# Field rows of a tile numbered 3i+r in place of 39r+i, with a separate load for the transposes

## What is computed

```
e  = stack([tbl_f[ids[:, f]] for f in range(39)], axis=1)          # 512 x 39 x 16
x1 = einsum('bid,bjd,ijh->bhd', e, e,  W0.reshape(39, 39, 128))    # 512 x 128 x 16
x2 = einsum('bid,bjd,ijh->bhd', e, x1, W1.reshape(39, 128, 128))
z  = sum(concatenate([x1, x2], axis=1), axis=-1)                   # 512 x 256
h  = maximum(concatenate([z, dense_ctx], 1) @ W_top1 + b_top1, 0)
h  = maximum(h @ W_top2 + b_top2, 0)
y  = h @ W_top3                                                    # 512 x 1
```

## Time and profile before

| | us |
|---|---|
| median of 3 runs | 597.44 (595.48 to 598.78) |
| profiled execution, its own time | 593.85 |
| its span in the trace | 592.0 |
| TensorE busy | 285.3 (48%) |
| VectorE busy | 168.1 (28%) |
| ScalarE busy | 137.9 (23%) |
| GpSimd busy | 154.1 (26%) |

### The profile page before, as it was taken

One profiled execution on the slowest core, in us unless ns is written; L12 is line 12 of the kernel. 1 busy time (PEld: TensorE's weight loads), 2 busy tenths in 40 slices (PEclk: granted clock), 3 DMA queues, 4 the chain that ended last, 5 costly groups with the idle time before them and its releaser, 6 DMA issues.

```text
span 592.0 us, 3817 instructions
## 1 busy us (share of the span) xinstructions
PE 285.3 (48%) x1132; PEld 219.6 (37%) x1132; DVE 168.1 (28%) x267; ACT 137.9 (23%) x252; POOL 154.1 (26%) x164
## 2 busy tenths in 40 slices
PE   3132450542617182643717183754736272746588
PEld 1011240331405172532615072642634161635367
DVE  4032230231414142231413142232414042232400
ACT  2011130230413122231413122231403122231421
POOL 6777733205060513214060513314000000000000
PEclk9999995575655557696955767685657577685879
DMA  3242255232232222222222222223212121122100
GB/s 75 45 109 64 76 141 120 79 98 67 80 60 80 57 81 56 78 66 68 77 60 79 54 81 57 80 67 74 72 57 81 50 79 51 76 64 74 67 0 2
DMA packets 59450, 41.50 MB, mean 70 GB/s; under 512 B 37323, under 2 KB 42699, under 8 KB 59430
## 3 DMA queue, kind: packets, MB, share of 16 engines
q1 hardware_dynamic: 54310, 39.94, 22.1%
q0 software_dynamic: 5120, 1.32, 3.8%
HBM read 36.65 MB, written 1.97 MB: 65 GB/s over the span
## 4 chain that ended last, share of the span: by engine, by line
SPq 86%; PE 4%; DMA 4%; issue 3%; POOL 2%; ACT 1%; DVE 0%; DVEq 0%
SPq L261 41%; SPq L286 17%; SPq L248 14%; SPq L247 8%; DMA second<-fields 3%; SPq L258 2%; SPq L272 2%; PE tower L542 2%; POOL gathered L310 2%; SPq L267 1%; SPq L271 1%; SPq L274 1%; PE tower L560 0%; DMA fields<-gathered 0%; SPq L275 0%
## 5 line engine op out<-in xcount | busy, mean ns | idle before, releaser
L310 POOL DMA_INDIRECT gathered<-table,rows x160 | 153.9, 962 | 254.1 <-DMA fields<-gathered 205.7
L340 DVE TENSOR_TENSOR prod<-first,second 117x512 f32<-117x512 f32 x112 | 77.6, 693 | 380.4 <-issue 194.8
L403 ACT CAST prod_hi<-prod 117x512 fp32r<-117x512 f32 x112 | 69.2, 618 | 244.2 <-DVE prod L340 244.2
L512 PE MATMUL sums<-prod_hi,w_hi 117*128 117x512 f32 x112 | 73.5, 656 | 101.6 <-DVE prod_lo L348 101.4
L497 PE MATMUL ring<-ident_f,first 39*128 39x39 f32 x64 | 10.3, 309 | 187.7 <-DMA first<-fields 187.7
L497 PEld LDWEIGHTS ring<-ident_f,first 39*128 39x128 f32 x64 | 8.0, 211 | 194.7 <-DMA first<-fields 194.7
L512 PEld LDWEIGHTS sums<-prod_hi,w_hi 117*128 117x128 f32 x112 | 28.7, 256 | 132.9 <-DVE prod_lo L348 100.4
L348 DVE TENSOR_TENSOR prod_lo<-prod,prod_hi 117x512 fp32r<-117x512 f32 x112 | 76.7, 685 | 0.1
L542 PE MATMUL tower<-dots,w_sb 128*128 128x128 f32 x312 | 62.1, 338 | 0.0
L542 PEld LDWEIGHTS tower<-dots,w_sb 128*128 128x128 f32 x312 | 59.0, 250 | 6.2 <-issue 0.2
L513 PE MATMUL sums<-prod_lo,w_hi 117*128 117x512 f32 x112 | 59.3, 529 | 0.0
(11 more groups left out here) (77 smaller groups left out, 157.5 us busy)
## 6 DMA issues: line engine op xcount, KB each, us to landing
second<-fields SPq DMA_DIRECT2D x112, 234.0 KB
first<-fields SPq DMA_DIRECT2D x16, 234.0 KB
gathered<-table,rows POOLq DMA_INDIRECT x160, 3.4
diag<-columns SPq DMA_DIRECT2D x128, 20.0 KB, 1.9
fields<-gathered SPq DMA_DIRECT2D x16, 80.0 KB, 10.1
wt_sb<-wt SPq DMA_DIRECT2D x2, 512.0 KB, 10.8
fields<-gathered SPq DMA_DIRECT2D x16, 40.0 KB, 10.2
w0a<-w_ij SPq DMA_DIRECT2D x1, 409.5 KB
```

The source lines that it names most:

```text
L310: pool.indirect_dma_start(gathered[:, k % NGATHER, q, :], None, table, bass.IndirectOffsetOnAxis(ap=rows[:, k, q:q + 1], axis=0)).then_inc ...
L340: nc.vector.tensor_tensor(prod[:, m % NPROD, :], first[:, k % 2, :], second[:, k % 2, t, :], ALU.mult)\
L403: nc.scalar.copy(prod_hi[:, m % NPART, :], prod[:, m % NPROD, :]).then_inc(hi_ready, 1)
L512: pe.matmul(to, w0_hi[:, t, :], hi, start=(t == 0), stop=False)
```

## The change

The rows of a tile are numbered p = 3i + r. In DRAM, the source of a tile load is described by three nested counts. Before, the outermost count is 3 (r) and the next 39 (i); in the change the outermost is 39 and the next 3. The destination has 117 partitions in both, and the bytes and the number of runs of 2 KB are the same. Row i of `first` was field i for the first 39 rows, and the transposes read these. Now three rows in a row hold the same field, so a ninth load of 39 rows, `turned`, brings the fields once more for the transposes; it is issued behind the load of tile 0. To make room for it, NGATHER is 3 in place of 4. The weight rows are sorted on the host by the new table.

```diff
@@ pair_tiles
-            i, shift = p % FIELDS, RUN * t + p // FIELDS
+            i, shift = p // RUN, RUN * t + p % RUN
@@ build
-        NPROD, NPART, NGATHER, NRING = 5, 7, 4, 4
+        NPROD, NPART, NGATHER, NRING = 5, 7, 3, 4
+        turned = sb("turned", [FIELDS, 2, COLS])
+        turned_in = [sem(f"turned_in{i}") for i in range(2)]
@@ load_pairs
                 sp.dma_start(first[:, at, :],
-                             bass.AP(fields.tensor, row, [[0, RUN], [COLS, FIELDS], [1, COLS]])).then_inc(first_in[at], 16)
+                             bass.AP(fields.tensor, row, [[COLS, FIELDS], [0, RUN], [1, COLS]])).then_inc(first_in[at], 16)
                 for t in range(TILES):
                     sp.dma_start(second[:, at, t, :],
-                                 bass.AP(fields.tensor, row + RUN * t * COLS, [[COLS, RUN], [COLS, FIELDS], [1, COLS]]))\
+                                 bass.AP(fields.tensor, row + RUN * t * COLS, [[COLS, FIELDS], [COLS, RUN], [1, COLS]]))\
                         .then_inc(second_in[t][at], 16)
+                    if t == 0:
+                        sp.dma_start(turned[:, at, :], bass.AP(fields.tensor, row, [[COLS, FIELDS], [1, COLS]]))\
+                            .then_inc(turned_in[at], 16)
@@ fields_by_column
-                pe.wait_ge(first_in[k % 2], 16 * (k // 2 + 1))
+                pe.wait_ge(turned_in[k % 2], 16 * (k // 2 + 1))
-                                      first[0:FIELDS, k % 2, P * s:P * s + P], ident_f[0:FIELDS, 0:FIELDS])
+                                      turned[:, k % 2, P * s:P * s + P], ident_f[0:FIELDS, 0:FIELDS])
```

## The result

| us | before | changed |
|---|---|---|
| median | 596.46 | 329.8 (328.04 to 332.64, 4 runs) |
| profiled execution, its own time | 593.85 | 328.04 |
| its span | 592.0 | 326.2 |

The ratio is 0.5533, with an interval of 0.5486 to 0.5579. The direction and the cause were forecast, the size was not: 284 was predicted, and 329.8 lies above the range of 262 to 316. On three later occasions the same kernel took about 400 us, as did most of its variants. So the ratio is that of one calm occasion out of four. All readings of the change itself come from undisturbed executions, or from blocks between spells.

What follows compares the result with a forecast made beforehand. The prediction took the kernel before as bound by eight tile loads draining at 3.2 us each. GpSimd's line to the last loads, 233.4, plus 14.3 + 30.6 + 3 gave 281.3, outside the span 283.2, forecast 284 us; range 262 to 316.

Steps and rivals of the forecast that it cites:

- part 1: Tile loads with 39 outermost: spread over 13 DMA engines in place of about three, 0.74 us a load for 3.2.
- 0.74 us a load: Drain of one tile load on 13 engines, 3.2 x 3/13; as long as its undisturbed issue of 0.69 to 0.76 us.
- at 288 a load takes 0.83: Rival: DMA engines at 288 GB/s or TensorE's waits set 15 to 15.5 us a block, 305 us in all; chance 0.12.
- the share of 0.97: DMA engines' busy share while the weights arrive, at 288 GB/s; read as 16 engines, the upper bound for tile loads.
- SyncE's sum of 13.5: SyncE's issues for one block: 12.7 us for fields, copies, tile loads and waits, plus 0.75 for the ninth load.
- L3: Start of block 3's tile loads on SyncE: forecast at 69.5 us, L2 + 13.5 + 2.
- L1: Start of block 1's tile loads on SyncE: forecast at 37.3 us, after its gathers landed at 30.9.
- L2: Start of block 2's tile loads on SyncE: forecast at 54 us, including two weight loads and fields behind them.
- is the bound by a hair: GpSimd's gathers, slowed beside VectorE, were to take 14.0 us a block, just over SyncE's 13.5.
- GpSimd held up fully: Rival: each gather waits out the VectorE operation it meets, 16.7 us a block, 321 us; 0.15 for 298 to 321.
- Part 2: Ninth load, for the transposes: 0.75 us of SyncE's queue, its landing hidden with 2.8 us to spare before the copies.
- Part 3: Three gather buffers: gathers wait for the fields of block k - 2 or k - 4, met by about a period; no cost.

Runs made afterwards that it cites:

- three_outer: Changed kernel with rows numbered 39r+i and 3 outermost again, ninth load and three gather buffers kept: 597.97 us, 1.0092 of the kernel before.
- half_columns: Changed kernel with tile loads bringing 256 of 512 columns from block 2 on: 399.84 us on a disturbed occasion, three blocks between spells 13.82 to 14.03 us.
- merged_wf: Changed kernel with tiles 1 to 6 in three transfers, weights issued before block 0, gathers always waiting for block k-3's fields: 325.4 us, 0.5466 of the kernel before.
- half_gathers: Changed kernel issuing five of a block's ten gathers from block 3 on: 327.45 us, 0.5511 of the kernel before.

## Why the prediction was wrong

**What bounded it, and part 1: right in the main.** "I take 13": the share of 0.82 in the loads' window is 13.1 engines, and with 3 outermost the gain is gone (`three_outer`). But the block was not "bound by the rate at which eight loads drain, 3.2 us each" alone: that is 25.6 us of 33.1. It was already a drain and then a row of short issues, the form that the changed kernel still has.

**The step that failed: 0.74 us a load, and "the queue runs full no longer".** The 3.2 x 3/13 keeps each engine at its pace, 75/3 = 25 GB/s. In the window 170 to 174 thirteen engines move 249 GB/s, 19 each. A load of 117 x 2 KB then drains in 0.96 us, while SyncE issues one in 0.83. The loads and the fields behind them are still draining when SyncE goes on, and line 250 and the copies are held: 2.1 us a block (`half_columns` against the changed kernel). Two things take the pace, counted in the packed traces: a packet of 2 KB occupies its engine for 98 ns in the mean in this window, and for 85 in that of the earlier trace rows; and 1.4 of the busy engines are taken by other packets, mostly those of the gathers. The Trainium skill (DMA: Bandwidth & Descriptors, section "Specifications") gives an engine about 27 GiB/s, from which an estimate for thirteen is 377 GB/s; the measured 249 decides.

The rival "at 288 a load takes 0.83" had the right mechanism, but too small: 15 to 15.5 us for 16.04. That it came nearer was in part luck with the window. The weights' stretch of the earlier trace rows is a mixture: of its 15.5 busy engines 10.8 carried the rows of 3,584 bytes of the weights on 117 partitions, and the rest shorter packets of other transfers. One us earlier, in the kernel before:

```profile
3.00:5.00 2.00, 0.00 (x0) 0.00 (x0) 0.23 (x3) 0.00 (x0) 1.22 (x2) 1.00 0.86 314
```

There 13.1 engines carried the weights' rows, 306 of the 314 GB/s. So these loads too ran on 13 engines and not on 16, which contradicts the prediction's reading of the share of 0.97; and at 306 a load of 117 x 2 KB would come out at 0.78 us, close to the forecast. Why thirteen engines do worse with the tile loads than with the weights, whether by the length of the rows or by the gathers beside them, no run here isolates.

**SyncE's sum of 13.5: low by 0.4.** It is 13.8 to 14.0 without holding. A tile load costs 0.83 where I had 0.76 with the gap to the next: the issue grew with the new pattern. With the 2.1 above, the period is 2.5 us longer than SyncE's forecast of 13.5, 12 x 2.5 = 30 us by the last block.

**The start: 69.5 forecast for L3, 86.2 measured.** L1 was 40.71 for 37.3: block 1's last gather took 5.7 us to land where 2.3 was taken, and landed at 34.30, not 30.9. From L1 to L2 it was 26.6 us for 16.7, from L2 to L3 18.9 for 15.5. Two terms of L2 were mis-sized, "1.5 (two weights)", which took 6.1 us, and "+ 2 (fields behind 2.5 MB of weights)", where the fields' two issues took 6.9 for 3.4:

```profile
48.60 0.87 SPq L276 DMA_DIRECT2D w_sb<-w  x1
49.93 4.77 SPq L277 DMA_DIRECT2D w_sb<-w  x1
54.75 4.66 SPq L249 DMA_DIRECT2D fields<-gathered  x1
59.46 2.19 SPq L250 DMA_DIRECT2D fields<-gathered  x1
```

```profile
49.00:60.00 11.00, 6.76 (x33) 5.01 (x31) 6.53 (x11) 6.11 (x11) 8.41 (x9) 0.97 0.96 268
```

All 16 engines are full for 11 us at 268 GB/s, and the queue is held for most of that time. With the weights at the start that goes (L1 to L2 15.8 in `merged_wf`, which also merges tile loads), and L3 comes 12 us earlier. 16.7 us of the miss lie here.

**GpSimd "is the bound by a hair": wrong.** SyncE was the bound, as `half_gathers` shows. The delay was taken as 0.2 for three gathers of four, 0.15 in the mean; the mean of 160 is 1.009, 0.07 over 0.94:

```profile
L315 POOL DMA_INDIRECT gathered<-table,rows x160 | 161.5, 1009 | 95.6 <-DMA fields<-gathered 47.2
```

A block of gathers is 13.1 us (ten of 1.009 + 0.30), which would have been under SyncE's 13.9 even without holding. By luck the forecast's 14.0 for GpSimd hid the error of SyncE's sum, which stood at 13.5 where 13.9 was true. The rival "GpSimd held up fully", 0.56 for such a gather, is further off still.

**Part 2, the ninth load: right in its cover, a little dear.** It costs 0.53 us for 0.75. The transposes wait long for it (89.0 us in all before line 502), but they end at 189.9, and the first copy of that block starts at 192.77. The chain that ended last does pass through its landing in two of the last twelve full blocks (3.75 us at 119.02, 3.45 at 248.82) and goes on over the products to the next `first`. These blocks took 16.0 and 15.7 us, no more than the others: SyncE and the computing engines were ready together. **Part 3: right.** SyncE waits for gathers twice, 19.5 us in all, both at the start. **TensorE: right.** The granted clock is 0.86 in the mean. Of the last twelve full blocks five have 1.00, with a mean period of 16.2, and seven 0.67 to 0.79, with 15.9, so the clock doesn't set the block; and two thirds of its tile work less change nothing. **The end: right.** From the last loads to the end of the span 47.6 us, forecast 14.3 + 30.6 + 3 = 47.9.

The account: 16.7 at the start and 12 x 2.5 = 30, less the 1.9 by which GpSimd's line lay over SyncE's in the forecast, is 45; the profiled execution missed by 328.0 - 283.2 = 44.8. (The last step of the sum has a small slip: 283.2 and 0.6% are 284.9, not 284.)

## What to carry to other kernels

When a transfer that ran on few DMA engines is spread, don't divide its time by the number of engines: take the GB/s of stretches of the same trace in which many of them are busy, several of them and with rows of the same length where there are any, and compare the drain of a whole burst with its issue time, not one load with one issue. If the drain is longer, a queue that takes all transfers in order is held at whatever comes next, and fewer, larger issues only move the wait. What helps is to put the small issues that follow the burst on another engine's queue, or large one-time loads ahead of the first block. And time such a kernel on several occasions before believing one number: this one took 330 us on one and about 400 on three.

## What was not expected of the hardware

- Thirteen DMA engines with 2 KB runs move 249 GB/s, where three moved 75: 19 for 25 GB/s an engine. A packet of 2 KB took 98 ns in the mean for 85. With the weights' rows of 3,584 bytes thirteen moved 306.
- The issue of a load of 117 rows costs SyncE 0.78 to 0.87 us with 39 outermost; before, 0.69 to 0.76. One that brings six tiles costs 0.81.
- SyncE is held by bytes that still drain: with half the bytes of the loads 2.1 us of a block's 16.0 go, and with six loads in one issue the next issue is held for 5 us more.
- Semaphore increments of TensorE can reach ScalarE 17 us late on some occasions, and on those over half of the records of semaphore updates are missing (3608 to 3833 of 8112).
